# Field-pair attention pooling on one core: the transposes of x on row-stacked operands

## The chip, the cores and the metric

The kernel runs on one core of one Trainium2 chip. The time is the device time of one execution in microseconds; it is given as a median of several runs. Engines are named as in the profile: PE is TensorE (its matmuls), PEld its weight loads, DVE is VectorE, ACT is ScalarE, POOL is GpSimd, SP is SyncE, which issues most of the DMAs.

## The reference

For each of 2048 batches, x has 39 fields of 64 numbers. All 741 pairs of fields are multiplied element by element, go through a hidden layer and a softmax over the pairs, and the weighted sum is projected to one number:

```python
row, col = np.triu_indices(F, k=1)
ip = x[:, row, :] * x[:, col, :]                       # 2048 x 741 x 64, fp32
hidden = relu(einsum('bpd,da->bpa', ip, W_w) + b_w)
logits = einsum('bpa,a->bp', hidden, W_h) + b_h[0]
a = softmax(logits, axis=1)[:, :, None]
return sum(a * ip, axis=1) @ W_p + b_p
```

## The kernel before

The work is done in 64 blocks (`BLOCKS`) of 32 batches, four steps each; four blocks make a group, for which one softmax is taken. Everything is fp32. Two batches, one of each half, form what the code calls a duo: after a transpose they lie on 128 partitions as two times 64 features, with the 39 fields as columns. A block has 16 duos, eight for each `u` of two (`ROW_DUOS` is 8, `BLOCK_DUOS` 16).

In each block:

- SP loads x for the block after the next but one (`load`, line 181): two DMAs, one for each `u`, each of 39 fields by 16 batches by 64 numbers, to the partitions 0 to 38 and 64 to 102 of `x_rows`. It waits until the last x has been transposed (`x_cols_ready`). Behind these DMAs on SP's queue come the eight of `write_gram` (lines 190 and 192), which wait for ScalarE's copy of the gram matrices, and every fourth block `load_values` (line 204).
- TensorE transposes x (`transpose`, line 472): 16 matmuls, each with the 39 rows and 128 columns of one duo as weights and the 39 by 39 identity as the moving operand. The two values of `u` lie on the two row tiles of the array (partitions 0 and 64), and are issued in turn. The result goes to slot 2 (`X_SLOT`) of `z` in PSUM, one bank for each `u`. The last of the 16 increments `x_cols_ready`.
- TensorE computes the gram matrices of the block (`gram_matrices`, line 484), 32 matmuls (64 instructions) of 39 by 39 on four 64-row, 64-column tiles. `cross_work` calls both, once in each round of `block_work`, ahead of chunk 6; at the last block only the gram matrices are left, so the transposes of `cross_work` run 63 times.
- VectorE copies the transposed x to `x_wide` (`spread`, lines 304 and 305) once the gram matrices have been computed, and forms the products of the pairs (line 329, four per block). GpSimd scales x for the next gram matrices (line 278) and copies head weights (line 267).
- TensorE multiplies the products by the hidden weights in twelve chunks (`hidden_layer`, line 529, eight matmuls or 16 instructions each, 64-row and 32-column tiles), ScalarE rectifies them (line 407), and TensorE forms the logits in two halves a step (line 549). The order is written out by hand in `block_work`.

The first block is different: `FIRST_X` splits its x into three DMAs (line 208), which are transposed with the same function as they land, on one row tile at a time. The identity is built at the start on GpSimd (lines 255 and 259), once for each row tile.

Of the kernel before, what the change touches and what calls it, by code (L numbers as in the profile page):

```python
# [5 lines left out]
def bass_pairwise_attention_pooling(  # L6
# [27 lines left out]
    ALU = mybir.AluOpType  # L34
# [3 lines left out]
    BATCHES, FIELDS, D = x.shape  # L38
    A = w_hidden.shape[1]
    P = 2 * D  # L40
# [13 lines left out]
    ROW_DUOS = BLOCK_STEPS * QUADS // 2  # L54
    BLOCK_DUOS = 2 * ROW_DUOS
    ROWS = D + FIELDS
    TILE = 32
    assert GROUP_BLOCKS == 4 and GROUPS % 2 == 0

# [16 lines left out]
    def item(j, v=0):  # L76

        return j + (j >= cross_at(v))
# [3 lines left out]
    X_SLOT, GRAM_SLOT = 2, 1  # L82
    BEFORE_X, BEFORE_GRAM = 3, 4
    FIRST_X = ((0, slice(0, ROW_DUOS), 0), (0, slice(ROW_DUOS, 2 * ROW_DUOS), 1), (1, slice(0, 2 * ROW_DUOS), 0))

    x_rows_dram = x.rearrange("(v u b) f d -> u f v b d", v=BLOCKS, u=2)
    gram = nc.dram_tensor("gram", [BATCHES, FIELDS, WIDE], fp32, kind="Internal").ap()
    gram_blocks = gram.rearrange("(v u p h) i w -> h u i v p w", h=2, v=BLOCKS, u=2)
    gram_rows = gram.rearrange("(t q h) i w -> h q t (i w)", h=2, q=QUADS)
# [3 lines left out]
    with ctx:  # L93
        def sb(name, shape, dt=fp32):
            return ctx.enter_context(nc.sbuf_tensor(name, shape, dt))

        def ps(name, shape):
            return ctx.enter_context(nc.psum_tensor(name, shape, fp32))

        def sem(name):  # L100
            return ctx.enter_context(nc.semaphore(name))
# [5 lines left out]
        bp_col = sb("bp_col", [P, 1])  # L107
        head_cols = sb("head_cols", [P, 2, TILE + GROUP_STEPS - 1])
        head_w = sb("head_w", [P, BLOCK_STEPS, 2, TILE])
        ident = sb("ident", [ROWS, FIELDS])  # L110
        x_rows = sb("x_rows", [ROWS, 2 * ROW_DUOS, D])
        x_wide = sb("x_wide", [P, BLOCK_DUOS, WIDE])
        x_scaled = sb("x_scaled", [P, BLOCK_DUOS, FIELDS])
        prod = sb("prod", [P, BLOCK_STEPS, QUADS * PAIRS])
# [13 lines left out]
        z = ps("z", [P, 3, 2, BANK])  # L128
# [8 lines left out]
        ident_ready = sem("ident_ready")  # L137
        first_x_loaded = [sem(f"first_x_loaded{i}") for i in range(3)]
        x_loaded = sem("x_loaded")
        x_cols_ready = sem("x_cols_ready")  # L140
# [36 lines left out]
        def _(sp):  # L177
            def load(v):
                sp.wait_ge(x_cols_ready, v + 2)
                for u in range(2):  # L180
                    sp.dma_start(x_rows[u * D:u * D + FIELDS, :, :],
                                 x_rows_dram[u, :, bass.ds(v, 1), :, :]).then_inc(x_loaded, 16)

            def write_gram(v, slot):
                sp.wait_ge(z_read, ITEMS * v + cross_at(v) + 1)
# [19 lines left out]
                            "p (i k) -> p i k", k=OFFSETS), bands).then_inc(values_loaded[slot], 16)  # L205

            for i, (u, batches, _) in enumerate(FIRST_X):
                sp.dma_start(x_rows[u * D:u * D + FIELDS, batches, :],  # L208
                             x_rows_dram[u, :, 0, batches, :]).then_inc(first_x_loaded[i], 16)
            for h in range(2):  # L210
                rows = slice(h * D, (h + 1) * D)
# [41 lines left out]
        @block.gpsimd  # L253
        def _(pool):
            nc.gpsimd.memset(ident[:, :], 0.0).then_inc(ident_ready, 1)
            pool.wait_ge(ident_ready, 1)
            for j in range(2):
                one = ident[j * D:j * D + FIELDS, :]
                nc.gpsimd.affine_select(out=one, in_=one, compare_op=ALU.not_equal, fill=1.0, base=0,
                                        pattern=[[-1, FIELDS]], channel_multiplier=1).then_inc(ident_ready, 1)  # L260
                pool.wait_ge(ident_ready, j + 2)

            def place_heads(step):

                pool.wait_ge(logits_done, step - BLOCK_STEPS + 1)
                at = GROUP_STEPS - 1 - step % GROUP_STEPS
                nc.gpsimd.tensor_copy(head_w[:, step % BLOCK_STEPS, :, :],  # L267
                                      head_cols[:, :, at:at + TILE]).then_inc(head_w_ready, 1)

            def scale_x(v):  # L270

                pool.wait_ge(x_spread, 2 * (v + 1))
                if v == 0:
                    pool.wait_ge(act_spread, 4)
                    pool.wait_ge(cols_loaded, 16 * N_COLS)
                else:
                    pool.wait_ge(z_ready, ITEMS * (v - 1) + CROSS_AT + 1)
                nc.gpsimd.tensor_scalar(x_scaled[:, :, :], x_wide[:, :, 0:FIELDS], wp_col[:, 0:1], None,  # L278
                                        ALU.mult).then_inc(x_scaled_ready, 1)

            scale_x(0)
            pool.wait_ge(head_cols_loaded, 16 * 4)
            for step in range(BLOCK_STEPS):
                at = GROUP_STEPS - 1 - step
                nc.gpsimd.tensor_copy(head_w[:, step, :, :], head_cols[:, :, at:at + TILE]).then_inc(head_w_ready, 1)
            for step in range(BLOCK_STEPS, STEPS):
                if step % BLOCK_STEPS == 0:
                    scale_x(step // BLOCK_STEPS)
                place_heads(step)
# [101 lines left out]
        def _(act):  # L391
# [18 lines left out]
            def copy_gram(v, slot, writes):  # L410

                act.wait_ge(z_ready, ITEMS * v + cross_at(v) + 1)
                if not (isinstance(writes, int) and writes == 0):
                    act.wait_ge(gram_written[slot], 16 * GRAM_DMAS * writes)
                nc.scalar.copy(gram_out[0:ROWS, slot, :, :, :],  # L415
                               z[0:ROWS, GRAM_SLOT, :, 0:XCOLS].rearrange("p u (d f) -> p u d f", f=FIELDS)
                               ).then_inc(z_read, 1)
# [45 lines left out]

        @block.tensor
        def _(pe):
            def transpose(slot, tiles=range(2), duos=range(ROW_DUOS)):

                for d in duos:
                    for u in tiles:
                        rows = slice(u * D, u * D + FIELDS)  # L470
                        duo = x_rows[rows, 2 * d:2 * d + 2, :].rearrange("f h d -> f (h d)")
                        last = nc.tensor.matmul(z[:, slot, u, FIELDS * d:FIELDS * (d + 1)], duo, ident[rows, :],  # L472
                                                is_transpose=True, start=True, stop=True, tile_position=(u * D, 0))
                last.then_inc(x_cols_ready, 1)

            def gram_matrices(v):
# [11 lines left out]

            def cross_work(v):

                pe.wait_ge(x_loaded, 32 * (v + 1))
                pe.wait_ge(z_read, ITEMS * v + item(BEFORE_X) + 1)
                nc.tensor.sem_inc(z_claimed, 1)
                transpose(X_SLOT)
                gram_matrices(v)

            def claim_slot(v, j, with_x):
# [19 lines left out]
            def hidden_layer(v, j, with_x=True):  # L517
# [6 lines left out]
                nc.tensor.sem_inc(z_claimed, 1)  # L524
                for a in range(0, A, TILE):
                    for b in range(2):
                        for h in range(2):
                            row, col, first = h * D, (h ^ b) * A + a, 2 * PAIRS * b + CHUNK * k
                            last = nc.tensor.matmul(z[col:col + TILE, SLOT[j], b, 0:CHUNK],  # L529
                                                    w_tiles[row:row + D, col:col + TILE],  # L530
# [63 lines left out]
                    cross_work(v + 1)  # L594
                chunks(6)

            pe.wait_ge(ident_ready, 3)
            for i, (u, batches, slot) in enumerate(FIRST_X):
                pe.wait_ge(first_x_loaded[i], 16)
                transpose(slot, (u,), range(batches.start // 2, batches.stop // 2))  # L600
            pe.wait_ge(w_loaded, 16 * 4)
            for j in range(CROSS_AT):
                hidden_layer(0, j)
# [40 lines left out]
```

## Time and profile before

| | |
|---|---|
| time, median of 3 runs (lowest to highest) | 1095.86 us (1095.33 to 1097.68) |
| profiled execution: time, span | 1094.35 us, 1092.6 us |
| PE, PEld busy | 1070.6 us (98%), 538.0 us (49%) |
| DVE, ACT, POOL busy | 956.4 us (88%), 872.1 us (80%), 858.7 us (79%) |
| mean granted clock of TensorE | 0.997 |

The span is from the first to the last instruction, and the time has a little around it. Busy times are shares of the span. The granted clock is 1 at 2.4 GHz and 0.5 at 1.2 GHz; the profile also lists 1 for the first 10 us, for which it has no record of the clock. The ends of matmuls are modelled, so their starts say more than their ends.

### The profile page before, as it was taken

Reading aid. Unit: us, or ns where it says so; the run is one execution under the profiler, and the core shown is the slowest. Engines: PE = TensorE matmul, PEld = TensorE weight load, DVE = VectorE, ACT = ScalarE, POOL = GpSimd, SP = SyncE. Lnnn points to the kernel's source line nnn. Section 1 sums busy time; section 2 is a strip of 40 time slices with the busy share of each in tenths; the row PEclk is TensorE's granted clock in tenths of the full one; section 3 lists DMA queues with packets and bytes.
Section 4 is the critical chain, followed back from the end, with each engine's and each line's share of the span. In section 5 each row is a group of like instructions: output and inputs, shape, how many; then the busy total and the mean of one; then the engine's idle time right before and its main releaser. Section 6 shows DMA issues by size and latency. Waiting matters only on the chain.

```text
span 1092.6 us, 60354 instructions
## 1 busy us (share of the span) xinstructions
PE 1070.6 (98%) x25856; PEld 538.0 (49%) x25856; DVE 956.4 (88%) x484; ACT 872.1 (80%) x884; POOL 858.7 (79%) x327
## 2 busy tenths in 40 slices
PE   8999999999999999999999999999999999999995
PEld 4544445445545455444455554544554545445542
DVE  8989898898998988988988889889889899898991
ACT  6788787888877878878788888888788787887874
POOL 7887787787787877877878878778787788787781
PEclk9999999999999999999999999999999999999998
DMA  3344363434544244362552634635444344434422
GB/s 50 45 38 45 38 43 45 46 35 45 36 45 56 25 45 47 34 59 23 46 55 24 59 37 40 49 32 48 44 37 45 41 40 45 50 31 45 43 30 26
DMA packets 333445, 45.47 MB, mean 42 GB/s; under 512 B 333421, under 2 KB 333421, under 8 KB 333421
## 3 DMA queue, kind: packets, MB, share of 16 engines
q1 hardware_dynamic: 332973, 45.10, 43.1%
q8 instruction: 13, 0.21, 0.1%
q14 instruction: 11, 0.09, 0.0%
q10 hardware_dynamic: 448, 0.07, 0.0%
HBM read 26.59 MB, written 18.54 MB: 41 GB/s over the span
## 4 chain that ended last, share of the span: by engine, by line
PE 98%; issue 1%; DMA 0%; DVE 0%; ACT 0%; SPq 0%; DVEq 0%
PE z L529 60%; PE logits L549 30%; PE z L484 4%; PE z L472 4%; DMA x_rows<-in_r_x_dram 0%; PE logits L539 0%; ACT exps L430 0%; DVE neg_max L338 0%; DVE weighted L346 0%; SPq L208 0%; DVE exp_bias L340 0%; DVE y_all L352 0%; DVE inv_sum L349 0%; DVEq L351 0%; DVE pooled L346 0%
## 5 line engine op out<-in xcount | busy, mean ns | idle before, releaser
L407 ACT ACTIVATE hidden<-z,b_col 128x988 f32<-128x988 f32 x768 | 803.6, 1082 | 167.8 <-PE z L529 167.6
L329 DVE TENSOR_TENSOR prod<-x_wide 128x2964 f32<-128x2964 f32 (+1 forms) x257 | 845.6, 3340 | 7.4
L529 PE MATMUL z<-prod,w_tiles 64*32 64x494 f32 x12288 | 760.2, 576 | 2.5 <-issue 0.9
L267 POOL COPY head_w<-head_cols 128x64 f32<-128x64 f32 x252 | 522.5, 2103 | 66.2 <-PE logits L549 66.2
L278 POOL TENSOR_SCALAR x_scaled<-x_wide,wp_col 128x624 f32<-128x624 f32 x64 | 332.8, 5200 | 145.1 <-DVE x_wide L305 139.2
L549 PE MATMUL logits<-hidden,head_w 64*32 64x370 f32 (+1 forms) x8192 | 441.6, 472 | 4.4 <-issue 4.0
L529 PEld LDWEIGHTS z<-prod,w_tiles 64*32 64x32 f32 x12288 | 271.2, 106 | 246.0 <-issue 123.3
L549 PEld LDWEIGHTS logits<-hidden,head_w 64*32 64x32 f32 x8192 | 179.4, 106 | 239.9 <-issue 238.7
L304 DVE COPY x_wide<-z 128x624 f32<-128x624 f32 x63 | 51.0, 809 | 98.2 <-PE z L484 98.2
L415 ACT COPY gram_out<-z 103x624 f32<-103x624 f32 x64 | 43.4, 678 | 36.2 <-PE z L484 34.5
L472 PEld LDWEIGHTS z<-ident,x_rows 39*128 39x128 f32 x1024 | 38.1, 139 | 42.7 <-issue 41.5
L484 PE MATMUL z<-x_wide,x_scaled 64*39 64x39 f32 x4096 | 52.8, 202 | 0.5 <-issue 0.5
L472 PE MATMUL z<-ident,x_rows 39*128 39x39 f32 x1024 | 45.8, 233 | 4.4 <-DMA x_rows<-in_r_x_dram 4.2
L484 PEld LDWEIGHTS z<-x_wide,x_scaled 64*39 64x39 f32 x4096 | 45.3, 113 | 4.3 <-issue 1.3
L305 DVE COPY x_wide<-z 128x304 f32<-128x304 f32 x63 | 29.3, 465 | 0.0
L346 DVE CUSTOM_DVE_ANT_0 weighted<-exps,values 128x742 f32<-128x742 f32 x16 | 15.3, 957 | 1.0 <-ACT exps L430 1.0
L338 DVE TENSOR_REDUCE neg_max<-logits_copy 128x1 f32<-128x742 f32 x15 | 13.8, 919 | 0.0
L338 DVE TENSOR_REDUCE neg_max<-logits 128x1 f32<-128x742 f32 x1 | 0.9, 930 | 14.5 <-PE logits L549 14.5
L430 ACT ACTIVATE exps<-logits_copy,exp_bias 128x742 f32<-128x742 f32 x15 | 13.6, 903 | 0.0
L423 ACT COPY logits_copy<-logits 128x742 f32<-128x742 f32 x15 | 11.6, 777 | 0.0
L539 PEld LDWEIGHTS logits<-w_tiles 64*32 64x32 f32 x256 | 4.7, 104 | 10.8 <-issue 10.2
L352 DVE TENSOR_SCALAR y_all<-pooled,inv_sum,bp_col 128x1 f32 (+1 forms) x16 | 4.4, 273 | 4.2 <-DVE inv_sum L349 4.0
(22 smaller groups left out, 27.7 us busy)
## 6 DMA issues: line engine op xcount, KB each, us to landing
x_rows<-in_r_x_dram SPq DMA_DIRECT2D x127, 156.0 KB
gram<-gram_out SPq DMA_DIRECT2D x256, 47.5 KB
gram<-gram_out SPq DMA_DIRECT2D x256, 23.2 KB
values<-gram SPq DMA_DIRECT2D x128, 46.3 KB, 3.5
x_rows<-in_r_x_dram SPq DMA_DIRECT2D x2, 78.0 KB
out_dram<-y_all SPq DMA_DIRECT2D x8, 0.9 KB
w_tiles<-in_L_rec_W_w_dram ACTq DMA_DIRECT2D x4, 16.0 KB, 3.3
head_cols<-in_L_rec_W_h_dram SPq DMA_DIRECT2D x4, 0.2 KB, 2.3
```

Of the source, the lines that this page charges most:

```text
L267: nc.gpsimd.tensor_copy(head_w[:, step % BLOCK_STEPS, :, :], head_cols[:, :, at:at + TILE]).then_inc(head_w_ready, 1)
L278: nc.gpsimd.tensor_scalar(x_scaled[:, :, :], x_wide[:, :, 0:FIELDS], wp_col[:, 0:1], None, ALU.mult).then_inc(x_scaled_ready, 1)
L304: nc.vector.tensor_copy(wide[:, :, :, 0:FIELDS], cols).then_inc(x_spread, 1)
L305: nc.vector.tensor_copy(wide[:, :, :, FIELDS:WIDE], cols[:, :, :, 0:OFFSETS]).then_inc(x_spread, 1)
L329: nc.vector.tensor_tensor(out, one, other, ALU.mult).then_inc(ready, 1)
L346: nc.vector.tensor_tensor_reduce(out=weighted[:, :], in0=exps[:, :, :].rearrange("p b n -> p (b n)"), in1=values[:, slot, :], scale=1.0, s ...
L407: nc.scalar.activation(hidden[:, i, :, CHUNK * k:CHUNK * (k + 1)], z[:, SLOT[j], :, 0:CHUNK], ACT.Relu, bias=b_col[:, 0:1]).then_inc(z_rea ...
L415: nc.scalar.copy(gram_out[0:ROWS, slot, :, :, :], z[0:ROWS, GRAM_SLOT, :, 0:XCOLS].rearrange("p u (d f) -> p u d f", f=FIELDS)).then_inc(z ...
L472: last = nc.tensor.matmul(z[:, slot, u, FIELDS * d:FIELDS * (d + 1)], duo, ident[rows, :], is_transpose=True, start=True, stop=True, tile_ ...
L484: last = nc.tensor.matmul(z[col:col + FIELDS, GRAM_SLOT, u, FIELDS * d:FIELDS * (d + 1)], x_scaled[row:row + D, duo, :], x_wide[row:row + ...
L529: last = nc.tensor.matmul(z[col:col + TILE, SLOT[j], b, 0:CHUNK], w_tiles[row:row + D, col:col + TILE], prod[row:row + D, i, first:first + ...
L549: last = nc.tensor.matmul(logits[TILE * q:TILE * (q + 1), part, 0:cols], head_w[row:row + A, e, b, :], hidden[row:row + A, e, b, first:fir ...
```

## The change

The 16 matmuls of a block on two row tiles become six on the whole array. Three duos' rows lie below one another on 117 partitions (`STACK` is 3), so one matmul has 117 rows and 128 columns of weights and the 117 by 117 identity as moving operand, and gives the columns of three duos at once; the third matmul of each bank has two duos, 78 rows (`BANK_STACKS` is 3, 3, 2). The output goes to three runs of 39 columns, 117 columns apart. x is loaded by six DMAs a block instead of two, of 39 fields by 6, 6 and 4 batches. The first block keeps its row tiles and has a buffer and a function of its own. The identity has 117 rows and columns, built by one select.

```diff
+    STACK = 3
+    BANK_STACKS = (3, 3, 2)
...
+    stack_rows = STACK * FIELDS
...
-        ident = sb("ident", [ROWS, FIELDS])
-        x_rows = sb("x_rows", [ROWS, 2 * ROW_DUOS, D])
+        ident = sb("ident", [stack_rows, stack_rows])
+        first_x_rows = sb("first_x_rows", [ROWS, 2 * ROW_DUOS, D])
+        x_rows = sb("x_rows", [stack_rows, 2, 2 * STACK, D])
...
                 for u in range(2):
-                    sp.dma_start(x_rows[u * D:u * D + FIELDS, :, :],
-                                 x_rows_dram[u, :, bass.ds(v, 1), :, :]).then_inc(x_loaded, 16)
+                    for k in range(STACK):
+                        batches = slice(2 * STACK * k, min(2 * STACK * (k + 1), 2 * ROW_DUOS))
+                        sp.dma_start(x_rows[FIELDS * k:FIELDS * (k + 1), u, 0:batches.stop - batches.start, :],
+                                     x_rows_dram[u, :, bass.ds(v, 1), batches, :]).then_inc(x_loaded, 16)
...
-            for j in range(2):
-                one = ident[j * D:j * D + FIELDS, :]
-                nc.gpsimd.affine_select(out=one, in_=one, compare_op=ALU.not_equal, fill=1.0, base=0,
-                                        pattern=[[-1, FIELDS]], channel_multiplier=1).then_inc(ident_ready, 1)
-                pool.wait_ge(ident_ready, j + 2)
+            nc.gpsimd.affine_select(out=ident[:, :], in_=ident[:, :], compare_op=ALU.not_equal, fill=1.0, base=0,
+                                    pattern=[[-1, stack_rows]], channel_multiplier=1).then_inc(ident_ready, 1)
+            pool.wait_ge(ident_ready, 2)
...
-            def transpose(slot, tiles=range(2), duos=range(ROW_DUOS)):
+            def first_transpose(slot, u, duos):
 
                 for d in duos:
-                    for u in tiles:
-                        rows = slice(u * D, u * D + FIELDS)
-                        duo = x_rows[rows, 2 * d:2 * d + 2, :].rearrange("f h d -> f (h d)")
-                        last = nc.tensor.matmul(z[:, slot, u, FIELDS * d:FIELDS * (d + 1)], duo, ident[rows, :],
-                                                is_transpose=True, start=True, stop=True, tile_position=(u * D, 0))
+                    rows = slice(u * D, u * D + FIELDS)
+                    duo = first_x_rows[rows, 2 * d:2 * d + 2, :].rearrange("f h d -> f (h d)")
+                    last = nc.tensor.matmul(z[:, slot, u, FIELDS * d:FIELDS * (d + 1)], duo, ident[rows, rows],
+                                            is_transpose=True, start=True, stop=True, tile_position=(u * D, 0))
+                last.then_inc(x_cols_ready, 1)
+
+            def transpose():
+
+                for u in range(2):
+                    for d, stack in enumerate(BANK_STACKS):
+                        rows = FIELDS * stack
+                        duos = x_rows[0:rows, u, 2 * d:2 * d + 2, :].rearrange("f h d -> f (h d)")
+                        c0 = z[:, X_SLOT, u, FIELDS * d:FIELDS * d + 1]
+                        cols = bass.AP(c0.tensor, c0.offset, [c0.ap[0], [stack_rows, stack], [1, FIELDS]])
+                        last = nc.tensor.matmul(cols, duos, ident[0:rows, 0:rows],
+                                                is_transpose=True, start=True, stop=True)
                 last.then_inc(x_cols_ready, 1)
...
-                pe.wait_ge(x_loaded, 32 * (v + 1))
+                pe.wait_ge(x_loaded, 16 * 2 * STACK * (v + 1))
...
-                transpose(X_SLOT)
+                transpose()
```

## Rows read from the trace of the kernel before

**Rows 1.** The page: span, busy times, and the chain by engine.
```profile
span 1092.6 us, 60354 instructions
PE 1070.6 (98%) x25856; PEld 538.0 (49%) x25856; DVE 956.4 (88%) x484; ACT 872.1 (80%) x884; POOL 858.7 (79%) x327
...
PE 98%; issue 1%; DMA 0%; DVE 0%; ACT 0%; SPq 0%; DVEq 0%
```

**Rows 2.** Groups, whole span: busy us, mean ns | idle before them, releaser.
```profile
L529 PE MATMUL z<-prod,w_tiles 64*32 64x494 f32 x12288 | 760.2, 576 | 2.5 <-issue 0.9
...
L278 POOL TENSOR_SCALAR x_scaled<-x_wide,wp_col 128x624 f32<-128x624 f32 x64 | 332.8, 5200 | 145.1 <-DVE x_wide L305 139.2
L304 DVE COPY x_wide<-z 128x624 f32<-128x624 f32 x63 | 51.0, 809 | 98.2 <-PE z L484 98.2
L415 ACT COPY gram_out<-z 103x624 f32<-103x624 f32 x64 | 43.4, 678 | 36.2 <-PE z L484 34.5
L472 PEld LDWEIGHTS z<-ident,x_rows 39*128 39x128 f32 x1024 | 38.1, 139 | 42.7 <-issue 41.5
L484 PE MATMUL z<-x_wide,x_scaled 64*39 64x39 f32 x4096 | 52.8, 202 | 0.5 <-issue 0.5
L472 PE MATMUL z<-ident,x_rows 39*128 39x39 f32 x1024 | 45.8, 233 | 4.4 <-DMA x_rows<-in_r_x_dram 4.2
```

**Rows 3.** Windows of one block each: busy us of each engine, clock, DMA.
```profile
500.24:516.79 16.55, 16.52 (x402) 8.24 (x404) 15.62 (x7) 13.27 (x14) 14.52 (x5) 1.00 0.43 37
```

**Rows 4.** The chain, end of one block: start us, us, what.
```profile
507.05 0.83 PE z L529 x16
...
516.17 0.62 PE logits L549 x14
516.79 0.62 PE z L472 x16
517.41 0.75 PE z L484 x64
```

**Rows 5.** Timeline, end of one block: start us, us, engine, operation.
```profile
516.72 0.58 PEld L472 LDWEIGHTS z<-ident,x_rows 39*128 39x128 f32 x16 [0.60 <-issue]
...
517.34 0.82 PE L484 MATMUL z<-x_wide,x_scaled 64*39 64x39 f32 x64
```

**Rows 6.** Timeline of the first 14 us.
```profile
3.41 0.50 PEld L472 LDWEIGHTS z<-ident,x_rows 39*128 39x128 f32 x4 [3.41 <-issue]
...
5.62 0.93 PEld L472 LDWEIGHTS z<-ident,x_rows 39*128 39x128 f32 x8 [0.94 <-DMA x_rows<-in_r_x_dram]
...
8.50 6.94 SPq L181 DMA_DIRECT2D x_rows<-in_r_x_dram  x4
...
13.87 0.57 PEld L472 LDWEIGHTS z<-ident,x_rows 39*128 39x128 f32 x16 [0.81 <-issue]
```

**Rows 7.** Groups of 5.5 to 6.65 us: busy us, mean ns | idle before.
```profile
L529 PE MATMUL z<-prod,w_tiles 64*32 64x494 f32 x4 | 1.0, 1029 | 0.0
L472 PEld LDWEIGHTS z<-ident,x_rows 39*128 39x128 f32 x8 | 0.9, 216 | 0.9 <-DMA x_rows<-in_r_x_dram 0.9
```

**Rows 8.** SP's queue over the start of a block.
```profile
501.04 0.86 SPq L181 DMA_DIRECT2D x_rows<-in_r_x_dram  x2
502.51 0.33 SPq L190 DMA_DIRECT2D gram<-gram_out  x1
503.02 0.34 SPq L192 DMA_DIRECT2D gram<-gram_out  x1
```

**Rows 9.** Waits of SP's queue: us in total, times, longest.
```profile
SPq L181 <- PE z L472: 544.7, 62, 12.2
```

**Rows 10.** Windows of 1 us; the last two columns are DMA share, GB/s.
```profile
509.00:510.00 1.00, 1.00 (x32) 0.44 (x24) 1.00 (x2) 0.64 (x2) 1.00 (x1) 1.00 0.07 2
```

**Rows 11.** The page's DMA issues: KB each, median us to landing.
```profile
values<-gram SPq DMA_DIRECT2D x128, 46.3 KB, 3.5
```

**Rows 12.** The identity's operations: ns min/median/max, first and last start.
```profile
L259 POOL TENSOR_SCALAR_AFFINE_SELECT ident<-ident x2: 212/214/217, 1.1 to 1.4; 39x39 f32<-39x39 f32 x2
```

More of the change, by code:

```diff
@@ L86, in bass_pairwise_attention_pooling @@
     x_rows_dram = x.rearrange("(v u b) f d -> u f v b d", v=BLOCKS, u=2)
+    stack_rows = STACK * FIELDS
+    assert sum(BANK_STACKS) == ROW_DUOS and stack_rows <= P
     gram = nc.dram_tensor("gram", [BATCHES, FIELDS, WIDE], fp32, kind="Internal").ap()
@@ L207, in _ @@
             for i, (u, batches, _) in enumerate(FIRST_X):
-                sp.dma_start(x_rows[u * D:u * D + FIELDS, batches, :],
+                sp.dma_start(first_x_rows[u * D:u * D + FIELDS, batches, :],
                              x_rows_dram[u, :, 0, batches, :]).then_inc(first_x_loaded[i], 16)
@@ L595, in block_work @@
                 chunks(6)
-            pe.wait_ge(ident_ready, 3)
+            pe.wait_ge(ident_ready, 2)
             for i, (u, batches, slot) in enumerate(FIRST_X):
                 pe.wait_ge(first_x_loaded[i], 16)
-                transpose(slot, (u,), range(batches.start // 2, batches.stop // 2))
+                first_transpose(slot, u, range(batches.start // 2, batches.stop // 2))
             pe.wait_ge(w_loaded, 16 * 4)
```

## The prediction

> **What bounds the kernel now.** I read the page's first part, then its chain, then one block on the timeline. TensorE is busy for 1070.6 of 1092.6 us and the chain that ended last lies 98% on it [rows 1]. VectorE (956 us), ScalarE (872) and GpSimd (859) have room, and the idle time ahead of their operations is put down to TensorE or to one another [rows 1, 2]. TensorE's matmuls idle 2.5 us ahead of the hidden layer and 0.5 us ahead of the gram matrices in the whole span, so nearly every nanosecond that leaves TensorE's queue in a block leaves the time [rows 2]. Its granted clock is 1.00 in the blocks, the 2.4 GHz level [rows 3].
>
> In the chain one block reads: twelve hidden-layer chunks at 0.83 us, eight logit halves at 0.62, the transposes 0.62 and the gram matrices 0.75 [rows 4]. From one transpose stretch to the next are 16.55 us [rows 3]. So the changed stretch is 0.62 of 16.55 us, 3.7%. It runs 63 times: 1024 transposes in all [rows 2] less the 16 of the first block, by 16. The most that could be won is 39 us; what matters is the pace of the six.
>
> **The pace of a transpose now.** In a steady block the 16 weight loads begin at 516.72 and the last ends 0.58 us later; one takes 0.139, so from the first to the last start are 0.44 us, for seven further pairs (the two row tiles run beside one another): 63 ns a pair [rows 2, 5]. At the start a hidden-layer matmul takes 1029 ns where its mean is 576, so TensorE is at its lower level of 1.2 GHz there [rows 2, 7]; eight transposes sit in one row tile: from the first load to the end of the last 0.93 us, one 0.216, so 0.71 for seven steps, 0.10 a step, 0.107 when a first shorter step is allowed for [rows 6, 7]. 0.107 us are 128 cycles of 1.2 GHz, and at 2.4 GHz 128 cycles are 53 ns, with 9 to 10 more in the row. The loads bring 128 columns each, the matmuls stream 39. So I read the pace as that of a 128-column pass, the weight load, with the matmul hidden behind the load of the next one.
>
> Is it hidden? At 1.2 GHz 39 columns at one cycle each take 33 ns; in a row after the load they would make 139 a step, and the rows have 107. The gram matrices say the same: 64 instructions on four tiles leave 16 on each, and 0.82 less 0.20 over 15 steps is 41 ns, while a load of 39 columns (16 ns) and a fp32 matmul of 39 columns at two cycles (33 ns) would make 49 one after the other [rows 2, 5]. That a plain fp32 matmul takes two cycles a column in each of its two instructions, four in all, is seen in the chunks: 16 instructions on eight tiles are two a tile, and 0.83 us for the two is 0.41 for 494 columns, 2.0 cycles of 2.4 GHz a column [rows 4, 5].
>
> How many cycles a column a transpose takes is not shown; it is one instruction, not two [rows 2], and at 107 ns a step for 39 columns it can be at most 3.3. I bound it from both sides: one cycle (117 columns: 49 ns) and two, as the plain matmul's (98 ns). Three would be 146. I take one: the record of a transpose is 229 to 233 ns beside the gram matmul's 202, which streams the same 39 columns at two cycles on an array part of 39 columns instead of 128 [rows 2]; the 89 further array columns are 37 ns at one a cycle, which is more than the 28 to 31 of difference, so the transpose's own stream should be shorter than the gram's 33 ns, under two cycles a column. That is an argument about modelled ends, not proof.
> TensorE: Matmul & The Clock Gate, in the Trainium skill (Terms, the entry on the buses), says the transpose mode is four times faster for fp32, which from the four cycles a column seen above makes one. No run here shows it; by it the sum is the one below, and at two cycles it would be rival A's.
>
> **The change, part by part.** *Transposes.* Before, from the first transpose to the first gram matmul: 0.62 us [rows 4, 5]; seven steps of 0.063 are 0.44, so the last pair to the first gram is about 0.16 to 0.18 (drain and change of tile shape). After: six loads of 128 columns, with 117, 117, 78, 117, 117, 78 columns streamed. At one cycle a column the stream (49 ns, with 9 more as in the row 58) is below the load's 63, so five steps are 0.315; the last has 78 columns instead of 39, 0.016 more, then the same 0.16 to 0.18: 0.49 to 0.51. The array is now taken whole and given back to 64-row tiles; the changes of shape that are there now cost near 0.1 us (the gram matrices have 0.75 us in the chain for 16 steps of 0.041, 0.66) [rows 4], and are as many after; what can be added is the way through 128 array rows instead of 64, an estimate of 27 ns at one row a cycle. I allow 0 to 0.03 and take 0.02: 0.52. Saving 0.10 us a block, 63 blocks: 6.3 us. Bounds at this reading: 0.135 (nothing for the shape) gives 8.5, 0.08 gives 5.
>
> *Loads.* Six DMAs of 39 rows instead of two, the same bytes and 256-byte runs. SP issues the two in 0.86 us; the gram writes start 0.5 us apart, and at that pace six take about 3 us, so the gram writes behind them on SP's queue begin some 1.5 to 2 us later (now SP is free at 501.90 and waits to 502.51 for the gram copy) [rows 8]. Who waits: the gram buffer is used again two blocks later, and SP sits idle 545 us over 62 blocks ahead of the loads [rows 9]. DMA traffic has fallen to a share of 0.07 by 510 in a block that ends at 516.8 [rows 10], so 6 us of slack cover 2: nothing. The last two blocks load nothing, so the tail is untouched. At the start load(1) is issued at 8.50 and used at 13.87 [rows 6]: six issues end near 8.5 + 5 x 0.5 + 0.3, 11.3, and a landing up to 3.5 us later, as the reads of the gram matrices have it [rows 11], makes 14.8 at most: 0 to 0.9 us late, once. I take 0.2.
>
> *Identity.* One select over 117 columns in place of two of 0.21 us, and a wider memset; the last starts at 1.4 us, while the first transpose waits for x until 3.4 [rows 6, 12]. Three times a select's 0.21 from 1.1 on is 1.8: nothing, with 1.6 us of cover.
>
> *What follows.* The gram matrices begin 0.10 us earlier, so VectorE's copies, GpSimd's scaling and ScalarE's copy do too; each of these waits for them now (98.2, 139.2 and 34.5 us in all) [rows 2], and VectorE's 1.6 us a block of wait is far over 0.1. No new wait.
>
> **The sum.** 6.3 less 0.2 is 6.1 us: 1088.3 on the profiled execution's own time. The profiled execution took 1094.35 us (1092.6 the span and 1.75 around it), 1.5 below the median 1095.86. On the median: 1089.8 us.
>
> **The rivals.**
> *A, two cycles a column.* The 117-column matmuls then set the pace: 98 ns and some 4 to 9, the 78-column one 69 to 74. Four and one are 0.48 to 0.50, the last transpose's stream is 0.033 longer, the tail 0.16 to 0.18, the shape 0 to 0.03: 0.67 to 0.74, against 0.62. Slower by 0.05 to 0.12 a block, 3 to 7.5 us: 1101. For it: the plain fp32 matmul's two cycles. Against: the length of the records. It decides from about 1.6 cycles a column on.
>
> *B, loads and matmuls one after the other.* 53 + 49 + 9 are 111 ns a step, 95 behind a 78-column one: 0.54 for five, with the last column count and the tail 0.72 to 0.73: some 6.6 us slower, 1102.5. The gap at which nothing is won is about 85 to 88 ns. Against: 107 ns at 1.2 GHz and 41 in the gram matrices, above.
> TensorE: Matmul & The Clock Gate, of the Trainium skill (Part 3, What overlaps and what doesn't), lets a load overlap a running matmul only where the row group differs; all six now share every row group, and by that rule the change loses these 6.6 us. The single row tile at the start speaks against it: 0.93 us for eight [rows 6].
>
> *C, partly hidden.* With 39 columns the matmul is short beside the load, with 117 nearly as long, and a step may come to 75 to 85 ns: the saving is then 0 to 0.04 a block, 0 to 2.5 us, within 0.2%: 1094.7.
> The same page's Back-to-back issue gap has about 81 ns a matmul for a stream of loads and 128-column matmuls; by an estimate from it five steps are 0.405 and the change wins 1 us. No row here shows it.
>
> *D, x late.* If the last of the six landed more than 6 us later than the last of the two, TensorE would wait in every block; 0.2 us of wait a block would cost 12.6 us, less the 6: 1102.5. The DMA share falls to nothing with 6 us left [rows 10], against 2 us of later issue.
>
> **How the numbers follow.** 0.2% is 2.2 us, about what a measurement of this kernel can tell from no change. My reading 0.66, A 0.13, B 0.06, C 0.13, D 0.02. My reading spans 1087.3 to 1091.8, all of it faster. A, B and D are slower, 0.21, of which a small part of A lies within 0.2%; C within, but for a tenth of it. So faster 0.67, same 0.13, slower 0.20. The range reaches from 1087.2 to 1100.0: it holds my reading, C and the lowest quarter of A, and leaves out some 2 in 10. The likeliest case's own range is 1087.3 to 1091.8.
>
> **What would show it.** The chain's transposes x6 at 0.50 to 0.53 us where they were 0.62, gram matrices still 0.75, blocks at 16.45 us. Loads some 63 ns apart: right; 80 is C, 100 and 74 in turn is A, 111 is B. SP's loads x6 over about 3 us and no wait of TensorE on x. The prediction is wrong if the stretch is not shorter, or if the 0.10 returns as idle time behind the gram matrices.

## The result, and the profile after

The change makes the kernel slower: 1109.17 us (1106.38 to 1111.94, four runs) against 1096.69 of the kernel before beside it (1095.33 to 1097.68, four runs). The ratio is 1.0106, 95% interval 1.0080 to 1.0133; of 1096.69 us that is some 11.6 us (8.8 to 14.6). The forecast was 1089.8 with a range of 1087.2 to 1100.0. The profiled execution took 1109.48 us, its span is 14.8 us longer than before.

The page after, its first part and the groups that answer to [rows 1, 2] (busy us, mean ns | idle us before them, releaser):

```profile
span 1107.4 us, 59728 instructions
...
L545 PE MATMUL z<-prod,w_tiles 64*32 64x494 f32 x12288 | 761.0, 576 | 3.2 <-issue 1.1
...
L488 PEld LDWEIGHTS z<-ident,x_rows 117*128 117x128 f32 x378 | 36.2, 141 | 38.1 <-issue 38.1
...
L500 PE MATMUL z<-x_wide,x_scaled 64*39 64x39 f32 x4096 | 53.4, 202 | 1.6 <-issue 1.5
...
L488 PE MATMUL z<-ident,x_rows 117*128 117x117 f32 x378 | 48.0, 262 | 0.0
```

Nothing here looks 14 us dearer. The hidden layer's mean is still 576 ns, the gram matrices' still 202, the matmuls of the transposes are 378 where they were 1024 and have no idle time ahead of them, so in the blocks x is never late. Groups add up records, and a record is not a place in time. So I went to one block. The window from one transpose stretch to the next, whose row before is [rows 3]:

```profile
505.99:522.83 16.84, 16.79 (x398) 8.24 (x391) 15.69 (x7) 13.27 (x14) 14.53 (x5) 1.00 0.21 37
```

It is 0.29 us longer at the same clock, with the same busy time on ScalarE and GpSimd. The chain of the block, whose rows before are [rows 4] (start us, us, what):

```profile
505.44 0.62 PE logits L565 x16
506.06 0.69 PE z L488 x6
506.75 0.75 PE z L500 x64
507.50 0.05 issue
507.54 1.06 PE z L545 x16
508.61 0.82 PE logits L565 x16
509.42 0.83 PE z L545 x16
510.25 0.62 PE logits L565 x16
```

In the kernel before, the rows behind those of [rows 4] are:

```profile
518.16 0.03 issue
518.18 1.06 PE z L529 x16
519.25 0.62 PE logits L549 x15
```

Two rows are new. The transposes have 0.69 us where they had 0.62. And the first logit half behind the gram matrices has 0.82, where it had 0.62 and every later one still has 0.62. This second row belongs to work that the change doesn't touch. The timeline of the same place, after:

```profile
505.99 0.58 PEld L488 LDWEIGHTS z<-ident,x_rows 117*128 117x128 f32 x6 [0.60 <-issue]
505.99 0.76 PE L488 MATMUL z<-ident,x_rows 117*128 117x117 f32 x6
...
506.93 2.83 SPq L188 DMA_DIRECT2D x_rows<-in_r_x_dram  x6
...
507.54 1.06 PE L545 MATMUL z<-prod,w_tiles 64*32 64x494 f32 x16
...
508.32 0.43 PEld L565 LDWEIGHTS logits<-hidden,head_w 64*32 64x32 f32 x16 [0.60 <-issue]
508.56 0.86 PE L565 MATMUL logits<-hidden,head_w 64*32 64x371 f32 x16
```

and before, behind the gram matrices of a block:

```profile
501.63 1.06 PE L529 MATMUL z<-prod,w_tiles 64*32 64x494 f32 x16
...
502.41 0.23 PEld L549 LDWEIGHTS logits<-hidden,head_w 64*32 64x32 f32 x16 [0.60 <-issue]
502.46 0.86 PE L549 MATMUL logits<-hidden,head_w 64*32 64x371 f32 x16
```

From the chunk's first matmul to the first logit matmul are 0.83 us before and 1.02 after; below I call this distance *chunk to logits*. The first load of the logits is issued 0.78 us behind the chunk in both; the 16 loads take 0.43 us instead of 0.23, and the first matmul starts 0.24 behind the first load instead of 0.05. So the engine did not wait for hidden values (the first load of the 16 was on time); something comes late behind the first load.

Over blocks 2 to 63, from the starts of the single matmuls in the two traces:

```
us, sum over 62 blocks              before    after     difference
first transpose to chunk            90.7      95.6      +4.9
chunk to first logit matmul         61.5      69.4      +7.9
first logit matmul to transposes   885.5     885.0      -0.5
```

So the mechanism has two parts: 0.07 us in every block, and 0.2 us in three blocks of four (in every fourth, where a group begins, chunk to logits is 1.4 to 1.7 us in either kernel, and the 0.2 does not show in it). The two blocks behind the loop, which are written out, have 0.83 as before. The first transposes behind the first block begin at 14.23 us where they did at 13.87 [rows 6], and from the start of the last transposes to the end of the span are 42.4 us where there were 40.6. With the 12.3 us of the table that makes the 14.8 of the span. But these two ends vary from execution to execution: in those of the experiments the last stretch is 39.0 to 43.4 us. It is the blocks that tell the kernels apart.

### The profile page after: what moved, and what is told of

It is laid out like the page before. It is cut to its first block, busy times and chain, and to the rows that moved or that the text cites. A ratio compares the mean times of both kernels' runs of the same rounds, so it can differ in the third digit from the quotient of the medians.

```text
span 1107.4 us, 59728 instructions
## 1 busy us (share of the span) xinstructions
PE 1082.5 (98%) x25226; PEld 543.6 (49%) x25226; DVE 956.4 (86%) x484; ACT 872.6 (79%) x884; POOL 859.6 (78%) x326
## 4 chain that ended last, share of the span: by engine, by line
PE 98%; issue 1%; DMA 0%; DVE 0%; ACT 0%; SPq 0%; DVEq 0%
PE z L545 59%; PE logits L565 30%; PE z L500 4%; PE z L488 4%; DMA first_x_rows<-in_r_x_dram 0%; PE logits L555 0%; PE z L476 0%; ACT exps L435 0%; DVE neg_max L343 0%; DVE weighted L351 0%; SPq L215 0%; DVE exp_bias L345 0%; DVE y_all L357 0%; DVE inv_sum L354 0%; DVEq L356 0%
## 5 line engine op out<-in xcount | busy, mean ns | idle before, releaser
L565 PE MATMUL logits<-hidden,head_w 64*32 64x371 f32 (+1 forms) x8192 | 442.1, 473 | 5.8 <-issue 5.3
L565 PEld LDWEIGHTS logits<-hidden,head_w 64*32 64x32 f32 x8192 | 183.6, 106 | 246.0 <-issue 238.1
L488 PEld LDWEIGHTS z<-ident,x_rows 117*128 117x128 f32 x378 | 36.2, 141 | 38.1 <-issue 38.1
L488 PE MATMUL z<-ident,x_rows 117*128 117x117 f32 x378 | 48.0, 262 | 0.0
L435 ACT ACTIVATE exps<-logits_copy,exp_bias 128x742 f32<-128x742 f32 x15 | 13.6, 904 | 0.0
```

Of the source, the lines that this page charges most:

```text
L488: last = nc.tensor.matmul(cols, duos, ident[0:rows, 0:rows], is_transpose=True, start=True, stop=True)
L565: last = nc.tensor.matmul(logits[TILE * q:TILE * (q + 1), part, 0:cols], head_w[row:row + A, e, b, :], hidden[row:row + A, e, b, first:fir ...
```

## The experiments

Two questions came from this: what paces the six transposes, and what holds the first logits back. For the second the loop was the suspect: the logits in question are the first instructions behind the branch that closes the loop over blocks. I call *place* the number of the loop's first instruction in TensorE's compiled program. Before it is 478, after 458, because the first round, which is written out ahead of the loop, has ten transposes (20 instructions, a load and a matmul each) fewer. (The traces show the differences between places, in the number of records ahead of the loop; the numbers themselves are those of the compiled program.) Dummy transposes of the identity, issued ahead of the first x, move the place without touching the loop. N of them add 2N instructions:

```diff
+            pe.wait_ge(ident_ready, 1)
             pe.wait_ge(ident_ready, 2)
+            for _ in range(N):
+                nc.tensor.matmul(z[0:FIELDS, X_SLOT, 1, 0:FIELDS], ident[0:FIELDS, 0:FIELDS],
+                                 ident[0:FIELDS, 0:FIELDS], is_transpose=True, start=True, stop=True)
```

Single executions of the kernel before range from 1091.5 to 1098.5 us beside these runs. So where a run has one execution only (e4 and e6 to e16, and e18), its time says little, and its trace decides.

**First four runs** (before beside them: 1094.11 us).

e1: the changed kernel with N = 10, place 478.

> The changed kernel with one wait and ten dummy transposes of the identity (21 instructions, 20 more than the one they stand for) ahead of the first x on TensorE, where it waits for x anyway. They stand for the 20 instructions that the first cross work lost, so that TensorE's loops begin at the same instruction as in the kernel before. Theory (the 0.2 us between the first chunk's end and the first logit matmul of a block is instruction delivery after the loop's branch and hangs on where the loop stands): from the last hidden-layer chunk's first matmul to the first logit matmul 0.83 us again, blocks of 16.62 us, time 1099 to 1103. Rival (it comes from the shorter body or from the late DMAs): still 1.02 us and 1108 to 1110.

Measured: 1099.67 us, ratio 1.0042 (1.0024 to 1.0060), some 4.6 us. Window, chain and timeline of a block:

```profile
504.03:520.66 16.63, 16.59 (x397) 8.28 (x391) 15.49 (x7) 13.27 (x14) 14.33 (x5) 1.00 0.21 37
```

```profile
504.10 0.69 PE z L488 x6
504.79 0.75 PE z L500 x64
505.54 0.03 issue
505.57 1.06 PE z L545 x16
506.63 0.62 PE logits L565 x15
```

The transposes keep their 0.69 and the logits have their 0.62 back, although the loop is the same code. The two parts are separate, and this one is 0.07 us x 63 = 4.4 us, close to the 4.6 measured (2.6 to 6.6).

e2: the kernel before with N = 6, place 490.

> The kernel before with 12 more instructions ahead of the first x, so that its inner loop begins at instruction 490 of the file, which leaves the remainder 10 by 16 and by 32, as 458 does in the changed kernel. Theory (place of the loop by 16 or 32 instructions): the first logit matmul of a block comes about 0.2 us late with nothing else changed, time 1105 to 1109. If the place counts by 64 or more, or not at all: 1094 to 1097.

Measured: 1095.74 us, ratio 1.0002 (0.9989 to 1.0015), chunk to logits 0.83 us. The rival was right: not every place costs.

e3: the kernel before with its x loaded by six DMAs.

```diff
-                    sp.dma_start(x_rows[u * D:u * D + FIELDS, :, :],
-                                 x_rows_dram[u, :, bass.ds(v, 1), :, :]).then_inc(x_loaded, 16)
+                    for batches in (slice(0, 6), slice(6, 12), slice(12, 16)):
+                        sp.dma_start(x_rows[u * D:u * D + FIELDS, batches, :],
+                                     x_rows_dram[u, :, bass.ds(v, 1), batches, :]).then_inc(x_loaded, 16)
```

> The kernel before with x loaded by six DMAs (6, 6 and 4 batches for each u) and nothing else changed. Theory: off the path, 1095 to 1098 and blocks of 16.55 us. Rival (SP's later gram writes or the DMAs cost something): 1099 or more.

Measured: 1093.81 us, ratio 0.9997 (0.9982 to 1.0012), and the chain is that of before:

```profile
499.22 0.62 PE z L473 x16
499.85 0.75 PE z L485 x64
...
501.68 0.62 PE logits L550 x14
```

The loads cost nothing that can be measured.

e4: the changed kernel with every stack two duos high, so that each of the six has 78 rows and columns; four of the 16 duos of a block are left out.

```diff
-                    for d, stack in enumerate(BANK_STACKS):
+                    for d, stack in enumerate((2, 2, 2)):
```

> The changed kernel with six transposes of 78 rows and 78 columns (stacks of 2, 2, 2), so four of sixteen duos are left out. Theory (two cycles a streamed column on the whole array): steps of 72 ns behind the first in place of 100, the transposes in the chain 0.57 us instead of 0.69, blocks shorter by 0.11 us. Rival (a fixed cost of the whole array a matmul): steps stay near 100 ns.

Measured: 1101.52 us (one execution), the transposes 0.55 us in the chain:

```profile
504.54 0.55 PE z L488 x6
505.09 0.75 PE z L500 x64
```

Starts of the six matmuls from the first, in ns, medians over the blocks; the last column is the way from the sixth to the first gram matmul:

```
after, columns 117 117 78 117 117 78      0  157  257  329  432  531    +162
e4, six times 78                          0  125  192  260  327  395
before, first and last of 16 matmuls      0                     461     +159
```

A step behind 117 columns is 99 to 103 ns, behind 78 it is 67.5 in e4 (72 after): 39 columns make 32.5 ns, and at 2.4 GHz that is two cycles each. (In these transposes the rows are always as many as the columns, so the steps alone can't say which of the two is paid for. The prediction's chunks, 494 columns on 64 rows in 0.41 us, go by columns, and I read the transposes so too.) Rival B, load and matmul in a row, would have a step of 53 + 98 at two cycles a column, or at one cycle 53 + 49 + 9 = 111 and 95, a difference of 16; it is out. The first step is 57 ns longer than its column count explains, in both. The blocks are 16.62 us, 0.22 shorter than after's 16.84, where I had expected 0.11: 0.14 is the transposes', and 0.08 comes behind the chunk, where chunk to logits is mostly 0.92 to 0.96. So the wait behind the loop's branch has no fixed size.

**Next four runs** (before: 1094.86 us).

e5, the kernel before with N = 22, place 522:

> The kernel before with 44 more instructions (one wait and 22 dummy transposes less the one they replace) ahead of the first x: its inner loop begins at instruction 522, which is 64 more than the changed kernel's 458. Theory (the place counts by 64 instructions): the first logit matmul of a block 0.1 to 0.2 us late, blocks of 16.65 to 16.75 us, time 1102 to 1106. Rival (it counts by another number, or by the distance from the program's start): 0.83 us as before and 1093 to 1096.

e6, e7, e8: the changed kernel with N = 2, 4 and 7, places 462, 466 and 472:

> The changed kernel with its inner loop at instruction 462 instead of 458. Theory (a piece of the loop's head comes late when the jump lands near the end of a piece of program): the late matmul moves to another instruction of the head and the wait is of another size; from the chunk's to the first logit matmul anything but 1.02 us. Rival (the place has no part in it): 1.02 us.

> The changed kernel with its inner loop at instruction 466. Theory: if the late piece begins at instruction 464, as the trace of the changed kernel puts it (the second instruction behind the jump's four is the late one), the head now lies wholly behind that border and the chunk's to the first logit matmul are 0.83 us. Rival: 1.02 us.

> The changed kernel with its inner loop at instruction 472, between 458 (late) and 478 (not late). Theory: 0.83 us, as at 478. Rival: 1.02 us.

Measured: e5 1092.95 us, ratio 0.9992 (0.9972 to 1.0012), chunk to logits 0.83: the rival again. e6, e7, e8 1101.16, 1100.33 and 1100.71 us, all with 0.83 from chunk to logits and blocks of 16.63 to 16.64. Two dummies, four instructions, are enough. In e6 the loads of the logits are back at

```profile
505.74 0.23 PEld L565 LDWEIGHTS logits<-hidden,head_w 64*32 64x32 f32 x16 [0.60 <-issue]
```

**Next four runs** (before: 1095.78 us). The dummies had moved the end of the loop too, by as much as its beginning. e9 puts four dummy transposes into the loop's own round, so its branch lies where it did in e7, while its beginning stays at 458:

```diff
+                if not (isinstance(v, int) and v == 0):
+                    for u in range(2):
+                        for _ in range(2):
+                            nc.tensor.matmul(z[0:FIELDS, X_SLOT, u, XCOLS:XCOLS + FIELDS], ident[0:FIELDS, 0:FIELDS],
+                                             ident[0:FIELDS, 0:FIELDS], is_transpose=True, start=True, stop=True)
```

> The changed kernel with four dummy transposes of the identity (eight instructions) behind the six, inside the loop only: the loop begins at instruction 458 as in the changed kernel, and its branch stands at 1295, as in the run whose loop begins at 466 and which was not late. Theory (the loop's place, not the branch's): the first logit matmul late again, near 1.02 us from the chunk, time 1108 or more (the dummies themselves cost 0.1 to 0.3 us a block). Rival (the branch's place): 0.83 us.

e10, e11, e12: N = 32, 8 and 64, places 522, 474 and 586:

> The changed kernel with its loop at instruction 522, 64 more than 458. If the place counts by 64 or a part of it: 1.02 us between the chunk and the first logit matmul, blocks of 16.84 us. If it counts by more, or by the absolute place alone: 0.83 and 16.63 us.

> The changed kernel with its loop at instruction 474, 16 more than 458. If the place counts by 16: 1.02 us, blocks of 16.84 us. Else 0.83 and 16.63 us.

> The changed kernel with its loop at instruction 586, 128 more than 458. If the place counts by 128 or a part of it: 1.02 us, blocks of 16.84 us. Else 0.83 and 16.63 us.

Measured: e9 1126.52 us; its four dummies are 0.27 us a block in its chain, and chunk to logits is 1.02 again:

```profile
516.40 0.27 PE z L514 x4
...
518.51 0.82 PE logits L570 x16
```

It is the beginning of the loop that counts, not the branch. e10, e11, e12 1099.09, 1102.45, 1102.70 us, all 0.83 (the 64 dummies of e12 put the first transposes behind the first block at 16.8 us). No period of 16, 32, 64 or 128 instructions, then.

**Next four runs** (before: 1098.54 us) around 458. In e13, e14 and e16 the first round alone leaves out two, one and four of its six transposes; e13 has two dummies, and so comes back to 458.

```diff
-            def transpose():
+            def transpose(left_out=0):
...
+                        if len(BANK_STACKS) * u + d < left_out:
+                            continue
```

> The changed kernel with the two dummy transposes of the run at place 462 and two of the six transposes of the first cross work left out (four duos of block 1 are stale), so that the loop stands at 458 again with the dummies in place. Theory (the loop's place): 1.02 us from the chunk to the first logit matmul. Rival (dummies ahead of the first x change something else): 0.83 us.

> The changed kernel with one transpose of the first cross work left out (three duos of block 1 are stale): the loop stands at 456. Theory (a stretch of late places below 462): late, 1.0 us or more between the chunk and the first logit matmul. Rival (458 alone, or the lack of change): 0.83 us.

> The changed kernel with one dummy transpose more: the loop stands at 460. Theory: between 458 (0.20 us late) and 462 (0.05 us late behind the branch, hidden by the chunk): 0.83 to 1.0 us from the chunk to the first logit matmul. Rival: 1.02 us as at 458.

> The changed kernel with four transposes of the first cross work left out: the loop stands at 450. Theory (a border in the loop's head that the code slides over): other instructions of the head are late than at 458, or none. Rival (every place below 462 is late alike): 1.02 us.

Measured: e13 (458) 1110.54 us and 1.02 us, its 16 loads of the logits in 0.43 us as in the changed kernel; dummies as such cure nothing.

```profile
509.00 0.43 PEld L567 LDWEIGHTS logits<-hidden,head_w 64*32 64x32 f32 x16 [0.60 <-issue]
```

e15 (460, one dummy) 1111.19 and 1.00. e14 (456) 1108.47 and e16 (450) 1110.81: both 0.83 from chunk to logits, and yet blocks of 16.83. What I had watched, the first logit matmul, is not what is late there. The single records tell it. Of four rounds three are entered by the branch back to the loop's beginning, 45 in an execution; the table has the medians over these, in ns after the start of the branch. At the loop's beginning stand register instructions, the wait (place + 4), and then loads and matmuls in turn, the first load at place + 5:

```
place                             wait  loads 1 to 6                  matmuls 1 to 3
478 (before), 586 (e12)           547   623 659 666 673 673 679       671 703 710
466 (e7)                          547   623 658 665 672 672 678       670 703 709
462 (e6)                          547   624 659 666 673 673 679       671 704 710
460 (e15)                         737   812 845 848 855 862 868       843 850 857
458 (after, e13), 714 (e18)       547   622 867 870 877 884 890       865 872 879
456 (e14)                         547   623 672 855 861 868 875       671 856 863
450 (e16)                         547   622 658 665 672 718 867       670 716 866
```

The first late load is the second at 458, the third at 456 and the sixth at 450: instruction 465 of the program each time, at 855 to 867 ns. (At e18's place, 714, the second load is the first late one as at 458, 256 instructions further on.) In single rounds it is mostly 853 or 868, and in e4, which has the same place 458, 785. At 460 it is the wait that is late, instruction 464. At 462, with 464 among the register instructions, 33 of the 45 rounds are on time; in 9 the wait and all behind it come 46 ns late, which the chunk that still runs mostly hides (chunk to logits 0.86 at most). So whatever lies from 464 on is held back behind that branch, and the loop's beginning slides over this border. (At 450 the third matmul, instruction 460, is late too; I have no reason for that.)

**Last two runs** (before: 1095.31 us). e17 takes the place alone: the kernel before, with 10 of the 16 transposes of the first round left out, so its loop begins at 458, with its own transposes.

```diff
+                        if 2 * d + u < left_out:
+                            continue
...
-                transpose(X_SLOT)
+                transpose(X_SLOT, left_out=10 if isinstance(v, int) and v == 0 else 0)
```

> The kernel before with ten of the sixteen transposes left out in the first cross work only (data of block 1 are stale), so that its loop stands at instruction 458, as the changed kernel's; every other block is as before. Theory (place): the first logit matmul of a block 0.2 us late, blocks of 16.74 to 16.77 us, the time 8 to 12 us above the kernel before. Rival (it takes the new transposes or loads too): 16.55 us, within 2 us of before.

e18, the changed kernel with N = 128, place 714 = 458 + 256:

> The changed kernel with its loop at instruction 714, 256 more than 458. If borders come every 256 instructions: late as at 458, blocks of 16.84 us (and some us more at the start for 128 dummies). Else 16.63 us.

Measured: e17 1101.37 us, ratio 1.0062 (1.0047 to 1.0076), some 6.8 us. A window, the chain and the timeline of it:

```profile
522.00:538.75 16.75, 16.72 (x408) 8.36 (x401) 14.50 (x6) 13.27 (x14) 13.67 (x5) 1.00 0.28 36
```

```profile
522.07 0.62 PE z L474 x16
522.69 0.75 PE z L486 x64
523.44 0.03 issue
523.47 1.06 PE z L531 x16
524.53 0.82 PE logits L551 x16
```

```profile
524.24 0.43 PEld L551 LDWEIGHTS logits<-hidden,head_w 64*32 64x32 f32 x16 [0.60 <-issue]
```

The old transposes at 0.62, and the new row at 0.82, in a kernel that has nothing of the change in its loop. In its steady blocks the 0.2 comes in part: 0.91, 1.02 and 0.86 us in turn, the second load of the logits at 757, 867 and 701 ns, 6.6 us over blocks 2 to 63 where the changed kernel has 7.9. So the time is up by less than the 8 to 12 us that I had expected. e18 took 1114.33 us, with 1.02 again, blocks of 16.84 and the chain

```profile
512.64 0.69 PE z L488 x6
513.33 0.75 PE z L500 x64
514.08 0.05 issue
514.12 1.06 PE z L545 x16
515.19 0.82 PE logits L565 x16
```

where e12 and e10, with fewer dummies, have 0.83. The border comes again 256 instructions on. The two parts add up to the whole: 4.6 us (e1) and 6.8 (e17, interval 5.1 to 8.3) beside 11.6. That they meet it within 0.2 us is luck, since each is known to some 2 us; the traces' own 4.9 and 7.9 say the same.

**Is it the fetching of the program from memory?** The profile lists the packets that bring instructions. The pages of before and of e17 have the same two lines for them (packets, MB, share of time):

```profile
q8 instruction: 13, 0.21, 0.1%
q14 instruction: 11, 0.09, 0.0%
```

Those of q8 have 16 KB each, and in e17 none of them lies between 37 and 1033 us, after the change none between 69 and 1038. From 70 to 1000 us, over 50 blocks, before and e17 have 8 packets on q14 alike, and the changed kernel and e1 have 35 alike, although e17 and the changed kernel are late and the other two are not. So as far as the profile lists them, no transfer from memory belongs to the late rounds.

## Why the prediction was wrong

*What bounds the kernel, and what a block is worth.* Right: both losses lie on TensorE's chain, and what is lost in a block is in the time. (One of the twelve chunks, the one behind the gram matrices, has 1.06 us in the chain and not 0.83; no sum used it.)

*"How many cycles a column a transpose takes ... I take one."* This step failed, and it is the one that turned the sign of the change as I had costed it: the stretch was to fall by 0.10 us a block, and rose by 0.07. It takes two: steps of 99 to 103 ns at 117 columns, 67.5 at 78. My evidence was the length of the records, whose ends are modelled. After, the matmuls with 117 and 78 columns have 262 ns where those with 39 had 233, 29 ns more for 65 columns more (117 and 78, two to one, are 104 on average), 0.45 ns or about one cycle of 2.4 GHz a column, while the starts show two. The fact that a plain fp32 matmul takes two cycles in each of its instructions was the better evidence, and I had written it down as rival A's.
TensorE: Matmul & The Clock Gate, in the Trainium skill (Terms, the entry on the buses), has the transpose mode four times faster for fp32; these steps against the four cycles of a plain matmul make it twice.

*Rival A's price* was right: 0.67 to 0.74 us for the stretch, 3 to 7.5 us, and it measured 0.69 and 4.6 (e1). Within it the sum differs: five steps are 0.53 us, of which 0.057 is the surplus of a first step that no term had (before, the first step was 84 ns and the others 62, which the average of 63 hid); the last transpose's longer stream, for which I added 0.033, added nothing (159 and 162 ns to the gram matrices), nor did the change of the tile's shape. The two errors are nearly equal, so that the price comes out so well is in part luck. The dummies of e9, 39 rows and columns on one tile, have steps of 38 to 39 ns at the same clock behind their first, where two cycles a column are 32.5 and one is 16: they are on A's side too.

*That the load is hidden behind the matmul before it* was right, with all six on the same rows of the array: a step is that of the stream alone, and rivals B and C are out.
What overlaps and what doesn't, Part 3 of that page of the Trainium skill, lets a load overlap only where the row group differs; the 100 ns steps here, where load and stream in a row would be 53 + 98, do not agree with it.

*Loads, x and SP.* Right: six DMAs take SP 2.83 us, I had about 3, TensorE waits for x in no block behind the first, and e3 puts their cost at 0.9997 (0.9982 to 1.0012). D is out. *Identity*: hidden, as forecast. I had 0.2 us for a later start. It came 0.36 later, but in e1, with the same six loads, it is at 13.87 us as before, and from 13.6 to 14.4 in the other runs but e12 and e18, so nothing of it can be put down to the loads.

*What no step had.* "The change part by part" costed fewer instructions at nothing and never asked where the rest come to lie. The ten transposes less in the round ahead of the loop move the loop's beginning from 478 to 458, ahead of a border at 464, and behind each branch the instructions past it are held back, at 458 until some 865 ns. That is 0.2 us in three blocks of four, 6.6 to 7.9 us, more than the whole gain that I had forecast. It is shown as far as this: it follows the loop's beginning and not its branch (e9), not the dummies (e13), not the change (e17); the first late load has the same number at 450, 456 and 458; it comes again at 256 on (e18), and not at 16, 64 or 128. The 256 suggests that the program is handled in pieces of this size. That a piece is fetched from memory in each late round is the first reading that comes to mind, and the packets above speak against it. What holds the instructions back is not shown.
Runtime: NRT & Kernel Launch, in the Trainium skill (Instruction fetch mechanics), has instructions fetched in blocks of 256, calls a crossing mostly hidden, and names a branch to a block that isn't there as a stall. The 256 agrees; that a fetch by DMA is what stalls, no run here shows. Here the branch's own target comes in time (the wait at 547 ns at every place but 460), and what is late is what lies behind the next border, within some 14 instructions of it.

What stays open: what holds the instructions past the border back, since the packets of instructions don't show it, and why until 785 ns in e4 and until 868 after; why the first step of the six is 57 ns longer than the rest; why e17 pays the 0.2 only in part of its rounds; and why a group's first logits come 1.4 to 1.7 us after their chunk in every kernel, which is more in a block than anything in this study. No version here beats the kernel before. Its six loads (e3) and its other places (e2, e5) are all the same within 0.2%.

## What to carry to other kernels

Stacking rows under a transpose doesn't shorten its moving operand: the identity grows with the stack, so 16 duos stream 624 columns either way, at two cycles each 520 ns on the whole array, where two row tiles stream half of that each beside one another and were bound by their loads, at 63 ns a pair. Read the cycles of an operation from the distance of starts of a run of it, never from the length of records. And when a loop with a branch gets slower by the same amount in operations that nobody touched, look at the first instructions behind the branch: a few instructions more or fewer ahead of the loop can give or take 0.2 us a round, so before a change's own cost is judged, put dummies in the place of what it took out ahead of the loop, and compare again.

## What the runs showed of the hardware

- A fp32 transpose streams at two cycles a column: 67.5 ns a step at 78 columns, 99 to 103 at 117, at a granted clock of 1.00 (e4, after; rows and columns are equal in each).
- On the whole array a weight load of 128 columns is hidden behind the matmul before it, though both use the same rows: 100 ns a step, where in a row they would be 53 + 98 (after).
- A loop whose first instructions straddle a border (464, and again 256 on, by e18) has those past it mostly 853 to 868 ns behind the start of the branch (785 in e4, 701 to 867 in e17) instead of 660 to 680. With the loop's beginning from 2 instructions ahead of the border (462) to 122 behind it (586), chunk to logits is 0.83 us as before. No packet of instructions goes with the late rounds.
- Three times as many DMAs for the same bytes, 2.83 us of SP's queue instead of 0.86 in a block of 16.6, changed nothing in the time (e3).
